# Softmax attention's front with a column of q or k per row, one-hot products to the scores' rows, and a later shift in the loop

## What is computed

```python
def layer_norm(x, gamma, beta):
    mu = jnp.mean(x, axis=-1, keepdims=True)
    var = jnp.mean((x - mu) ** 2, axis=-1, keepdims=True)
    return (x - mu) * jax.lax.rsqrt(var + EPS) * gamma + beta
def apply_rope(t):                       # t: heads x 1024 x 8
    tp = t.reshape(*t.shape[:-1], d // 2, 2)
    t0, t1 = (tp[..., 0], tp[..., 1])
    rot = jnp.stack([t0 * cos - t1 * sin, t0 * sin + t1 * cos], axis=-1)
    return rot.reshape(t.shape)
...
# q = rope(h Wq + bq), k = rope(h Wk + bk), v = h Wv + bv, 16 heads of 8
# out = softmax(q k^T / sqrt(8)) v Wo + bo; then the feed-forward part with W1, W2
```

## Time and profile before

| | us |
|---|---|
| median of 3 runs | 950.79 |
| lowest, highest | 949.54, 954.23 |
| the profiled execution, its own time | 951.02 |
| its span in the trace | 948.9 |
| busy: PE, DVE, ACT, POOL | 829.0, 661.9, 554.9, 197.5 |
| the loop, first to last maximum | 338.17 to 646.9 |
| mean granted TensorE clock | 0.943 of full speed |

### The profile page before, as it was taken

How to read it: one execution, slowest core, us unless ns; L and a number is a source line. 1 busy time by engine, 2 the same in 40 slices (tenths; PEclk the granted TensorE clock), 3 DMA queues, 4 the chain that set the end, 5 groups by cost and what they waited for, 6 DMA issues and landing times.

```text
span 948.9 us, 17393 instructions
## 1 busy us (share of the span) xinstructions
PE 829.0 (87%) x6621; PEld 530.8 (56%) x6621; DVE 661.9 (70%) x1288; ACT 554.9 (58%) x1205; POOL 197.5 (21%) x177
## 2 busy tenths in 40 slices
PE   5889937799999889999999999999995899895894
PEld 3579734599856543333332333333575598594694
DVE  5945883266477999999999999992427364566362
ACT  3442532255525856999999988899634254413252
POOL 0100037355500050000000000000112454204385
PEclk9999958899999999999999999999996799995898
DMA  4650001311130000000000000000230312000444
GB/s 122 192 151 1 2 14 53 114 57 35 38 88 1 1 1 1 2 1 2 1 2 2 1 2 1 1 2 1 93 87 15 94 37 73 1 1 31 125 38 69
DMA packets 54643, 36.86 MB, mean 39 GB/s; under 512 B 9138, under 2 KB 50162, under 8 KB 54546
## 3 DMA queue, kind: packets, MB, share of 16 engines
q1 hardware_dynamic: 47218, 25.98, 9.8%
q0 software_dynamic: 7344, 9.77, 4.4%
HBM read 22.31 MB, written 14.48 MB: 39 GB/s over the span
## 4 chain that ended last, share of the span: by engine, by line
PE 33%; DVE 32%; POOL 14%; issue 10%; ACT 4%; DMA 4%; SPq 1%; POOLq 0%; DVEq 0%; ACTq 0%
DVE arena L1635 22%; POOL slots L1148 7%; POOL results L1159 5%; PE psum L1719 4%; POOL results L1170 3%; PE psum L1688 2%; PE psum L1252 2%; ACT arena L1899 2%; PE psum L287 2%; PE psum L280 2%; PE psum L402 2%; PE psum L380 2%; PE psum L1782 2%; PE psum L1770 1%; PE psum L1617 1%
## 5 line engine op out<-in xcount | busy, mean ns | idle before, releaser
L1635 DVE TENSOR_REDUCE arena<-psum 128x2 f32<-128x1024 f32 x256 | 294.1, 1218 | 8.6 <-PE psum L1617 8.6
L1899 ACT ACTIVATE arena<-psum 128x512 f32<-128x512 f32 x512 | 266.7, 607 | 19.0 <-PE psum L1688 16.8
L1295 ACT ACTIVATE arena<-psum,arena 128x128 f32<-128x128 f32 x340 | 96.9, 368 | 122.4 <-PE psum L1262 65.6
L1719 PE MATMUL psum<-arena 128*32 128x256 f32 (+1 forms) x1920 | 159.6, 405 | 0.2 <-ACT expert_w L1880 0.2
L287 PE MATMUL psum<-la_wqkv,ident 128*128 128x384 f32 x342 | 127.3, 524 | 12.7 <-DMA la_bo<-in_L_attn_a_bo_dram 10.2
L1688 PE MATMUL psum<-arena 32*128 32x512 f16 x512 | 127.1, 385 | 1.8 <-ACT arena L1899 0.4
L1617 PE MATMUL psum<-arena 32*128 32x512 f16 x512 | 100.7, 385 | 17.2 <-DVE arena L1635 15.2
L287 PEld LDWEIGHTS psum<-la_wqkv,ident 128*128 128x128 f32 x342 | 66.7, 203 | 63.2 <-issue 15.8
L1148 POOL DMA_INDIRECT slots<-xn,arena x64 | 66.6, 1041 | 167.3 <-DVE arena L1372 148.7
L1252 PE MATMUL psum<-arena 128*128 128x128 f32 x680 | 96.8, 288 | 0.4 <-DVE arena L1453 0.3
L1262 PE MATMUL psum<-arena 128*128 128x128 f32 x680 | 90.2, 276 | 1.0 <-ACT arena L1295 1.0
(11 more groups left out here) (279 smaller groups left out, 1066.5 us busy)
## 6 DMA issues: line engine op xcount, KB each, us to landing
arena<-slots SPq DMA_DIRECT2D x19, 256.0 KB, 3.1
arena<-results SPq DMA_DIRECT2D x12, 256.0 KB, 4.2
slots<-blank SPq DMA_DIRECT2D x1, 2560.0 KB, 11.8
expert_w<-in_L_attn_b_w_dram SPq DMA_DIRECT2D x1, 2048.0 KB, 8.5
expert_w<-in_L_attn_b_w_dram SPq DMA_DIRECT2D x8, 256.0 KB, 4.8
expert_w<-in_L_ffn_W_dram SPq DMA_DIRECT2D x1, 2048.0 KB, 8.5
expert_w<-in_L_ffn_W_dram SPq DMA_DIRECT2D x8, 256.0 KB, 4.5
results<-arena POOLq DMA_INDIRECT x85, 2.3
```

The costliest lines, as they stand in the source:

```text
L1295: last = nc.scalar.activation(self.hT[:, p, c, :], ps[:, 2 + p, c * P:(c + 1) * P], self.func, bias=own[:, FF + c:FF + c + 1])
L1635: v.tensor_reduce(self.mx[:, h % 2, keys, qt, 2 * pair:2 * pair + 2], core.psum[:, 2 * slot:2 * slot + 2, :], AX.X, ALU.max).then_inc(self ...
L1719: last = nc.tensor.matmul(core.psum[32 * j:32 * j + 32, 7, cols], self.vs[:, b * TB + kt, HG * g + j, :], self.prob[:, k % self.PROBS, j, ...
L1899: nc.scalar.activation(self.prob[:, k % self.PROBS, j, :], core.psum[:, 4 + tile % self.SCORE_BANKS, :], ACT.Exp).then_inc(self.prob_in, 1)
```

## The change

- `Weights.sync` loads the biases of q and k as two columns (`sa_bqk`), and behind the clearing of `slots` writes the rope's cosines and sines with a row per column to DRAM: four copies with 4-byte elements to `angles` (L905 of the new file), a wait, and two copies that repeat them for the 16 heads to `tables`. `load_tables`, ahead of the softmax stage's other work on SP, loads them (1 MB) into `cos_sin`.
- POOL makes the one-hot matrices and the weights with swapped columns (partner columns, one with its sign turned) in ten steps, `prepare`, one behind each of the result scatters 4 to 13 of the third stage.
- The second channel mix's DVE work gets two small operations (`shift_rows`).
- The front is written anew, with 128 columns of q or k on the partitions and 1024 tokens of a batch along a row: PE makes the product with the weights and that with the swapped weights (`product`), DVE does `rotate` (three operations for q or k of one batch) and `take_low`, ACT `take_high`. One-hot products (`expand`, two for each 128 x 512, high and low part) give `qT` and `kT`, which ACT moves out, 512 columns at a time (`move_expanded`), for k with the constant 256 added. The first four expansions stand ahead of the ring, the other 28 between the ring's first fills, without `keep_busy`.
- ACT's constant fills of the q and k columns go; the fill of `m4` (`clear_maxima`) stands ahead of the second norm's square roots. The values get 16 columns per head in place of 32, so waves have 16 output rows.
- In the loop `AHEAD` is 5 (6), `SHIFT_AT` (4, 6) in place of (3, 6), the pairs of heads go in the order (0, 1) in place of (1, 0), the last half's waves are made whole, and a product with zeros clears bank 7 ahead of the first shift.

```diff
@@ Weights.sync
         sp.dma_start(self.slots.rearrange("(t p) d -> p t d", p=P),
                      self.blank[:, :].unsqueeze(1).to_broadcast([P, 40, D])).then_inc(self.slots_clear, 16)
+        rows = a["c_rope"].rearrange("p i t j -> j (i t) p")
+        for j in range(HD // 2):
+            sp.dma_start(self.angles[j, :].rearrange("(c p) -> c p", p=P), rows[j],
+                         allow_slow_non_contiguous=True).then_inc(self.angles_in, 16)
+        sp.wait_ge(self.angles_in, 8 * HD)
+        for e in range(2):
+            sp.dma_start(self.tables.rearrange("h (j e) n -> h j e n", e=2)[:, :, e, :],
+                         self.angles.unsqueeze(0).to_broadcast([H, HD // 2, 2 * S])).then_inc(self.tables_out, 16)
@@ Experts.gpsimd
                                     in_=self.y[:, t, :], in_offset=None).then_inc(w.result_out[t % LANES], 16)
+            if self.beside:
+                self.beside.prepare(pool, t)
@@ SoftmaxAttention
-    AHEAD = 6
-    SHIFT_AT = (3, 6)
+    AHEAD = 5
+    SHIFT_AT = (4, 6)
...
-        parts = [(qt, pair, keys) for qt in range(4) for keys in range(2) for pair in (1, 0)]
+        parts = [(qt, pair, keys) for qt in range(4) for keys in range(2) for pair in (0, 1)]
@@ wave
-        if kt == 0 and part == 1:
+        at_once = kt == 0 or h == self.HALVES - 1
+        if at_once and part == 1:
             return
...
-            last = nc.tensor.matmul(core.psum[32 * j:32 * j + 32, 7, cols], self.vs[:, b * TB + kt, HG * g + j, :],
+            last = nc.tensor.matmul(core.psum[32 * j:32 * j + 16, 7, cols], self.vs[:, b * TB + kt, HG * g + j, :],
@@ expand
+        core.claim(pe, turn)
+        pe.wait_ge(self.low_in, 2 * b + 2)
+        at = b * S + 512 * half
+        for a, part in enumerate((self.high, self.low)):
+            rows = (self.expand_q, self.expand_k)[which][:, a, HG * g:HG * g + HG, :].rearrange("p j r -> p (j r)")
+            last = nc.tensor.matmul(core.psum[:, turn.bank, :], rows, part[:, which, at:at + 512], start=(a == 0),
+                                    stop=(a == 1))
@@ loop_tensor
-        for i in range(8):
-            core.claim(pe, self.t[1]["qkT"][i])
-            keep_busy(core, self.w, pe, self.t[1]["qkT"][i].bank, 1)
-            self.turn_split(pe, 1, i)
-            self.ring_fill(pe, a)
-            self.ring_fill(pe, a + 1)
-            a += 2
...
+        for i in range(14):
+            for n in (2 * i, 2 * i + 1):
+                if n < 12:
+                    self.expand(pe, 0, 4 + n)
+                else:
+                    self.expand(pe, 1, n - 12)
             self.ring_fill(pe, a)
             a += 1
+            if i % 3 == 2:
+                self.ring_fill(pe, a)
+                a += 1
...
+        core.nc.tensor.matmul(core.psum[:, 7, :], self.w.blank[:, :], self.w.sa_w1[:, :], start=True, stop=True)
@@ tensor
+        self.turn_first(pe, 0)
+        for i in (0, 1, 2, 3, 7):
+            pe.wait_ge(core.emptied[i], self.before_products[i])
+        self.product(pe, 0, w.sa_wqkv[:, 1, :], 0)
+        self.product(pe, 0, self.swapped[:, 1, :], 2)
+        core.moved(pe, self.bias_turn)
+        self.product(pe, 0, w.sa_wqkv[:, 0, :], 6)
+        self.product(pe, 0, self.swapped[:, 0, :], 4)
+        pe.wait_ge(self.product_out, 1)
+        self.turn_first(pe, 1)
+        pe.wait_ge(self.product_out, 2)
+        self.product(pe, 1, w.sa_wqkv[:, 1, :], 2)
+        self.product(pe, 1, self.swapped[:, 1, :], 0)
+        pe.wait_ge(self.product_out, 3)
+        self.product(pe, 1, w.sa_wqkv[:, 0, :], 6)
+        pe.wait_ge(self.product_out, 4)
+        self.product(pe, 1, self.swapped[:, 0, :], 4)
+        pe.wait_ge(self.product_out, 6)
+        for i in range(4):
+            self.expand(pe, 0, i)
+        pe.wait_ge(self.product_out, 7)
+        self.values(pe, 0)
+        pe.wait_ge(self.product_out, 8)
+        self.values(pe, 1)
         self.loop_tensor(pe)
@@ scalar
         for g, turn in enumerate(self.t[0]["xT"]):
             self.move_tokens(act, turn, 0, g, 0)
+        self.clear_maxima(act)
         deviation(core, 1)
         deviation(core, 1, var=5, root=6)
@@ rotate, for k (which = 1) and then q (0) of a batch
+        dve.wait_ge(self.product_in, n + 1)
+        v.scalar_tensor_tensor(out=self.parts[:, 0, :], in0=self.core.psum[:, bank:bank + 2, :].rearrange(view),
+                               scalar=w.sa_bqk[:, which:which + 1], in1=self.cos_sin[:, 0, :], op0=ALU.add,
+                               op1=ALU.mult).then_inc(self.product_out, 1)
+        dve.wait_ge(self.product_in, n + 2)
+        v.scalar_tensor_tensor(out=self.parts[:, 1, :], in0=self.core.psum[:, partner:partner + 2, :].rearrange(view),
+                               scalar=self.swapped_b[:, which:which + 1], in1=self.cos_sin[:, 1, :], op0=ALU.add,
+                               op1=ALU.mult).then_inc(self.product_out, 1)
+        dve.wait_ge(self.product_out, n + 2)
+        v.tensor_tensor(self.turned[:, which, :], self.parts[:, 0, :], self.parts[:, 1, :],
+                        ALU.add).then_inc(self.turned_in, 1)
+        dve.wait_ge(self.turned_in, n // 2 + 1)
```

More of the change, by code:

```diff
@@ L1789, in loop_tensor @@
         core = self.core
-        first = self.t[0]["qkT"][0]
-        core.moved(pe, first)
-        keep_busy(core, self.w, pe, first.bank, 6)
         for i in range(4):
@@ new lines, in take_low @@
+    def take_low(self, dve, b, which):
+        v, ts = self.core.nc.vector, slice(b * S, (b + 1) * S)
+        dve.wait_ge(self.high_in, 2 * b + 2 - which)
+        if which:
+            v.tensor_tensor(self.low[:, 1, ts], self.turned[:, 1, :], self.high[:, 1, ts],
+                            ALU.subtract).then_inc(self.low_in, 1)
+        else:
+            v.scalar_tensor_tensor(out=self.low[:, 0, ts], in0=self.turned[:, 0, :], scalar=float(HD) ** -0.5,
+                                   in1=self.high[:, 0, ts], op0=ALU.mult, op1=ALU.subtract).then_inc(self.low_in, 1)
```

322 lines of the change are left out of this document (185 added, 137 removed).

## The result

The changed kernel takes 946.66 us (median of 15 executions, 942.47 to 955.54), the kernel before 950.94 (15, 948.79 to 954.23): a ratio of 0.9952, interval 0.9934 to 0.9970. That is 4.3 us faster where 9.9 were forecast, and just outside the range of 935.5 to 946.0. The profiled execution took 947.8, its span is 945.7.

What follows compares the result with a forecast made beforehand. DVE's own work was taken to bound the front and most of the loop, with ACT close behind. Terms -9.0 + 1.1 + 0.6 - 0.3 - 2.1 - 0.7 + 0.5 = -9.9 us gave 940.9, range 935.5 to 946.0.

Steps and rivals of the forecast that it cites:

- the last sentence of its working: Table writes: SP's queue is free from about 64 until the first gather at 176.64; no time was added.
- The rival on late tables: Single-element table writes delay SP's gather; at 16 ns an element the program is 24 us later, 965; chance 0.05.
- the ring's start: First 21 fills: shift starts one maximum earlier, 1.14 less, but DVE waits 1.4 for 0.57; net 0.3 us less.
- the last half: Loop's final half: a whole wave replaces two halves, 0.15 less in each of about five steps; 0.7 us less.
- DVE in the front: Second norm to first maximum: new DVE operations sum to 19.8 in place of 28.8; 9.0 us less.
- ACT ahead of the root: Fill of `m4` and scaling of `turner` delay the second norm's root, for which DVE waits; 1.1 us more.
- PE in the front: A PE gap of 2.8 us may halve the clock and delay expansions and values; 0.6 us more.
- The rival of a late PE: Clock halves through values and first expansions in the front, first maximum at 334 to 335; 944.5 us, chance 0.14.
- The loop: Softmax loop: DVE's 0.39 wait mostly moves behind the later shift, a half becomes 18.6; 2.1 us less, bounds 0 and 6.
- POOL: Ten small operations in POOL's idling between scatters may hold up DVE's weight copy; 0.5 us more, between 0 and 4.
- The 16 columns: Narrower values in the loop's waves: no gain by the profile rows, up to 0.1 us a half by shorter weight loads.

Runs made afterwards that it cites:

- the change with the constant: The changed kernel with the transposed angles as a constant in rows, without the four single-element transfers; 0.9935, 0.9922 and 0.9877 of the kernel before.
- constant_third: The changed kernel with the angles as a constant in rows, a repeat on another chip; 939.79 us, 0.9877 of the kernel before.
- root_first: The changed kernel with ACT's fill of `m4` and scaling of `turner` moved behind the second norm's roots; 948.22 us, 0.9951 of the kernel before.
- four_edits: Changed kernel with constant angles, `m4` fill behind roots, clearing product replacing busy ones, 22 busy products (not 20) before the linear memory's first norm; 944.57 us, 0.9879 of before.
- constant_guarded: Changed kernel with constant angles, two busy products in PE's gap before the expansions, POOL's additions behind DVE's first join; 941.24 us, 0.9879 of before.

## Why the prediction was wrong

**The step that failed** is the last sentence of its working, that the tables are written on SP's queue, "which is free from about 64 (52.4 + 11.8) until the first gather at 176.64", at a cost of nothing. It asked who waits for the tables and what queue they stand in, and never what shares the 16 engines below the queues. The rival on late tables looked at the same transfers and again only at their end: it put them at 2.3 ns an element and the point of danger at 13. They took 6.7 (from 52.8 until SP went on at 107.6), so the price of an element was nearly three times too low, but SP was free in time, as forecast, and the gather moved only with the scatters ahead of it. The harm was done on the way: beside the elements PE's signals came late, and the first scatter, to which the prediction gave no change, began 0.9 to 12 us late. It is worth an estimated 4.3 us in the means and 5.2 in the profiled pair. That the elements are the cause is shown by the runs with and without them; by what path they make the signals late stays open.

**Without it the time lies in the range, in part by luck.** 940.9 is 0.9896 of the kernel before; the change with the constant has 0.9911 in the mean of three. In its traces the softmax stage gains 11.1 to 11.4, but its medians lie only 7.5, 6.7 and 11.9 below before: on two of the chips some 4 us are lost outside the stage, and no run shows where. Within the stage two terms were off by about 1.5 each and cancel, the ring's start (+1.4 against its forecast) and the last half (-1.6).

Point by point:

- *DVE in the front, -9.0*: 28.8 became 19.6, -9.1. The choice of no surcharge for PSUM was right (1.28 a piece, as in the earlier trace rows).
- *ACT ahead of the root, +1.1*: DVE waits 1.5 more; taking it away gives 1.05.
- *PE in the front, +0.6*: the products were on time and the gap was 2.07, not 2.8. The clock stayed at 1.00 in the profiled execution, so the term is 0 there. The rival of a late PE did happen in single executions, at 0.5 plus 2.3 us; it had the mechanism and not what follows from it, the join behind POOL.
- *The ring's start, -0.3*: +1.1, the one term with a wrong sign. The step took the earlier start of the shift for a gain of 1.14. But a shift that starts one maximum earlier only moves this maximum of DVE's from ahead of the wait to behind it: the first fill behind the shift is read 25.8 after the first maximum, as before, and DVE then has four maxima to the join in place of three. What was right is the wait, 1.63 for a forecast 1.4.
- *The loop, -2.1*: -2.6. The period of 18.6 was met (18.58), with the waits behind both shifts. The four halves with outputs gained 0.2 each, and the odd join at the start 0.3.
- *The last half, -0.7*: -2.3, the right mechanism, mis-sized. The whole waves gave 1.55, where 0.15 in each of seven steps would be 1.05 and the forecast had counted five. The order gave 0.9, which wasn't counted. That scores start earlier behind a whole wave is a guess for the 0.5 that seven times 0.15 leave.
- *POOL, +0.5*: the experts' results took 72.30 us from the first scatter to the last, 72.09 before: +0.2. The copy L1462 went from 713 to 720 ns.
- *The 16 columns, nothing by the rows, up to 0.1 a half by the rule of the Trainium skill* (TensorE: Matmul & The Clock Gate, on LDWEIGHTS): the weight load did become shorter, 94 ns for 108, and a half gained 0.03 at most. The rule has the direction.

## What to carry over

A transfer that nobody waits for can still have a price when it is made of thousands of single elements: here 8192 of them delayed a stage that reads nothing of them. So look in the trace at what the engines do beside such a transfer, and lay a constant out in rows instead. Where the view says "remote" or "issue", compare the semaphore's time with the end of the instruction that sets it. An earlier release gains nothing as long as the same work is only moved from ahead of a wait to behind it; count the work on both sides. With the constant, the fill behind the root and the clearing product in place of the busy ones, the kernel takes 0.9863 and 0.9869 of before, where the change alone takes 0.9952, 0.9977 and 0.9938; on one chip (constant_third) the constant alone gave as much, 0.9877.

## What the runs showed of the hardware

- Beside single elements (4 bytes each, 8192 in four transfers) some of PE's signals came 1.9 to 5.7 us behind the products' modelled ends, in all six traces that have them, and DVE and ACT stood still for them; in the twelve others they came within 0.02. One load of 16 KB of instructions took 0.9 to 1.5 us elsewhere and 5.6 to 8.6 there. The time of the DMA packets counted over 1 while they moved 1 to 4 GB/s. The Trainium skill (SBUF — State Buffer, on who interferes with whom) says that DMA never contends with a compute engine. It says so of the memory's ports, and for those nothing here speaks against it; but these DMAs did hold up all three engines.
- A DVE operation of 0.16 us with its operands in SBUF took 2.12 and 2.14 when POOL's tensor operation had started just ahead of it, and ended with it. The Trainium skill has in the same section that such an operation with two SBUF inputs contends with a GpSimd instruction that reads SBUF, and that the port pair is an exclusive lock; the traces agree. Here 0.3 to 0.4 us of lateness decided whether it cost 0.2 or 2.0.
- TensorE at 1.2 GHz in one stretch cost 0.5 to 2.7 us, in other places in each execution (the start, the routing, PE's gap at 327, the linear memory). In the loop, 3.4 us at 1.2 GHz in root_first, four_edits and constant_guarded go with 276.9 to 277.1 from the third join to the last, where the changed kernel's order otherwise takes 275.6 to 275.7. Executions of one kernel on one chip differ by 3 to 7 us without the elements and by 4 to 14 with them, while a stage's time in the traces mostly repeats within 0.1: so a stage told more than a median.
